# Where the norms of three batches stand, and how the first item's front is cut: a Mamba, attention and expert kernel on one core

## The reference, cut to what matters

```python
x = x + attn(layernorm(x))            # two Mamba blocks, x is (4, 512, 256)
x = x + xattn(layernorm(x), ctx)      # cross attention
x = x + ffn(layernorm(x))             # shared expert and top-2 of 8 experts

# attn, for each of 2 layers:
xz = rmsnorm(x) @ in_w.T;  xb, z = split(xz)
xb = silu(conv4(xb) + cb)             # causal, 4 taps, 512 channels
delta, Bm, Cm = split(xb @ xp_w.T)    # 16 + 16 + 16
delta = softplus(delta @ dtw.T + dtb)
dA = exp(delta[..., None] * -exp(a_log));  mi = delta * Bm * xb
v = 0.6 * v + mi;  h = dA * h + v;  y = (h * C).sum(states)   # along the sequence
x = x + ((y + dp * xb) * silu(z)) @ out_w
```

## Time and profile before

| | us |
|---|---|
| median of three runs | 1530.66 |
| lowest, highest | 1529.70, 1532.19 |
| the profiled execution | 1527.98 |
| its span in the trace | 1526.5 |
| TensorE busy | 1373.7 (90%) |
| VectorE busy | 1056.8 (69%) |
| ScalarE busy | 898.0 (59%) |
| GpSimd busy | 926.8 (61%) |
| first scan starts | 73.8 |
| last scan ends | 948 |

### The profile page before, as it was taken

How to read it: one execution, slowest core, us unless ns; L and a number is a source line. 1 busy time by engine, 2 the same in 40 slices (tenths; PEclk the granted TensorE clock), 3 DMA queues, 4 the chain that set the end, 5 groups by cost and what they waited for, 6 DMA issues and landing times.

```text
span 1526.5 us, 46972 instructions
## 1 busy us (share of the span) xinstructions
PE 1373.7 (90%) x20570; PEld 972.8 (64%) x20570; DVE 1056.8 (69%) x1339; ACT 898.0 (59%) x1309; POOL 926.8 (61%) x809
## 2 busy tenths in 40 slices
PE   4679999999999999999999987789898887999997
PEld 2357677767767767777777765444434343599996
DVE  3299998798888887887986895676676761522224
ACT  3757767767766776786677663145555565434440
POOL 1269898989989989989989968500303000045441
PEclk8789999999999999999999998889999999999999
DMA  4111222221322212221221354540606001512225
GB/s 139 48 56 59 86 86 85 86 84 60 113 85 85 82 62 85 85 87 61 82 86 68 145 135 127 94 104 1 112 14 111 0 1 61 223 53 69 67 67 182
DMA packets 41498, 127.28 MB, mean 83 GB/s; under 512 B 8784, under 2 KB 21584, under 8 KB 32848
## 3 DMA queue, kind: packets, MB, share of 16 engines
q1 hardware_dynamic: 34736, 108.28, 21.8%
q0 software_dynamic: 6048, 14.95, 3.7%
q10 hardware_dynamic: 512, 1.05, 0.4%
HBM read 97.90 MB, written 9.57 MB: 70 GB/s over the span
## 4 chain that ended last, share of the span: by engine, by line
PE 47%; DVE 27%; ACT 10%; issue 8%; POOL 3%; DMA 3%; SPq 1%; DVEq 0%; ACTq 0%
DVE hst L783 12%; PE psum L635 6%; PE psum L614 4%; PE psum L1301 4%; PE psum L1713 4%; PE psum L1725 4%; DVE overlay L683 3%; DVE w_early L783 3%; PE psum L1283 2%; PE psum L576 2%; ACT dA L919 2%; PE psum L516 2%; POOL hst L990 2%; PE psum L1655 2%; PE psum L1267 2%
## 5 line engine op out<-in xcount | busy, mean ns | idle before, releaser
L990 POOL TENSOR_TENSOR hst<-hst,cb 128x512 f32<-128x512 f32 x399 | 510.9, 1304 | 99.0 <-DVE hst L783 84.2
L783 DVE TENSOR_TENSOR_SCAN hst<-dA,psum 128x512 f32<-128x512 f32 x399 | 463.4, 1201 | 119.5 <-PE psum L635 119.3
L614 PE MATMUL psum<-ident,hst 128*128 128x128 f32 x1596 | 238.2, 284 | 15.3 <-POOL hst L990 12.6
L919 ACT ACTIVATE dA<-delta,alog 128x512 f32<-128x512 f32 x256 | 177.7, 718 | 84.7 <-DVE hst L783 64.7
L614 PEld LDWEIGHTS psum<-ident,hst 128*128 128x128 f32 x1596 | 176.1, 143 | 62.4 <-issue 21.1
L919 ACT ACTIVATE dA<-xres,alog 128x512 f32<-128x512 f32 x256 | 176.3, 718 | 63.2 <-DVE hst L783 49.6
L1422 DVE TENSOR_REDUCE nmax<-psum 128x2 f32<-128x1024 f32 x128 | 154.7, 1220 | 57.4 <-PE psum L1267 57.1
L1351 ACT ACTIVATE pT<-psum 128x1024 f32<-128x1024 f32 x128 | 127.9, 1024 | 103.6 <-PE psum L1287 80.3
L635 PE MATMUL psum<-filt,c_early 64*64 64x86 f32 (+1 forms) x6144 | 147.3, 242 | 19.8 <-DVE hst L783 11.0
L635 PEld LDWEIGHTS psum<-filt,c_early 64*64 64x64 f32 x6144 | 126.7, 136 | 57.3 <-issue 38.6
L635 PE MATMUL psum<-filt,uT 64*64 64x86 f32 (+1 forms) x6144 | 145.1, 239 | 14.8 <-DVE hst L783 7.6
(11 more groups left out here) (231 smaller groups left out, 2108.9 us busy)
## 6 DMA issues: line engine op xcount, KB each, us to landing
cb<-c_rows SPq DMA_DIRECT2D x64, 1024.0 KB, 4.8
qk_first<-w_early SPq DMA_DIRECT2D x64, 64.0 KB, 2.4
qk<-part SPq DMA_DIRECT2D x64, 64.0 KB, 2.8
w_up<-up_dram SPq DMA_DIRECT2D x8, 512.0 KB, 7.5
w_down<-down_dram SPq DMA_DIRECT2D x8, 512.0 KB, 13.2
w_up<-y_choice SPq DMA_DIRECT2D x8, 512.0 KB, 6.7
qk<-part POOLq DMA_DIRECT2D x48, 64.0 KB, 5.1
qk_first<-part SPq DMA_DIRECT2D x40, 64.0 KB, 2.4
```

The costliest lines, as they stand in the source:

```text
L614: m = pe.matmul(psum[:, Y0 + et % EP, t * P:(t + 1) * P], hst(i)[:, t * P:(t + 1) * P], ident[:], start=n == 0 and t == 0, stop=n == NSTAT ...
L783: dve.tensor_tensor_scan(hst(i), a, v, 0.0, ALU.mult, ALU.add).then_inc(scan_done, 1)
L919: act.activation(dA[:, a % NDA, :], delta[k % 2][:, et, :], ACT.Exp, scale=alog[:, k // B, et, n:n + 1]).then_inc(decay_done, 1)
L990: pool.tensor_tensor(h, h, cb[:, q % 2, state_of(i)[1] % GN, :], ALU.mult).then_inc(g_done, 1)
```

## The change

`plan_norms` goes, and its work is put into `plan_first`. x_stats of batches 1 to 3 and x_aggr of both groups come on VectorE behind its last u. Both x_roots come on ScalarE behind the u copies, the x_recs behind them on VectorE, and one x_scale ahead of the copies of each of e1, e2 and e3. Silu of item 0 is four instructions, one for each channel tile; each waits for its convolution alone, and the xp products of a tile wait for its silu. `rates` comes straight behind silu. The chunk-end pieces of item 0 are shared: ScalarE copies those of even g, VectorE those of odd g (e1 three and three; e2 two 16x512, one 16x256 and one 16x512 on ScalarE, one 16x512 and one 16x256 on VectorE; e3 two and one). e2, e3 and the first filter products wait for VectorE's copies by a new semaphore `ends_dve`. Decays 0 to 2 stand on ScalarE between its e1 and e2 copies. Item 1's front takes the steps of the later items: xs at step 0, xn from step 2, p at steps 6, 9, 12, 14.

```diff
@@ plan_first
-                put("act", "silu")
+                for m in range(ET):
+                    put("act", "silu", m)
+                put("act", "rates")
@@
-                put("act", "rates")
@@
                     put("dve" if m % 2 else "pool", "u", m)
+                for b in range(1, B):
+                    put("dve", "x_stats", b)
+                for g in range(2):
+                    put("dve", "x_aggr", g)
@@
-                for part in STAGES:
+                for g in range(2):
+                    put("act", "x_roots", g)
+                    put("dve", "x_rec", g)
+                for b, part in zip(range(1, B), STAGES):
+                    put("dve", "x_scale", b)
                     for n in range(len(STAGES[part])):
                         put("pe", part, n)
                     s += 1
                     for n in range(len(STAGES[part])):
                         put("act", part, n)
+                        put("dve", "ends", (part, n))
+                    if part == "e1":
+                        put("act", "decays")
                     s += 1
@@ plan_front
-            def plan_front(k, at, start):
+            def plan_front(k, at):
-                xn_at = 2 if k > 1 else start + 2
-                p_at = (6, 9, 12, 14) if k > 1 else range(start + 5, start + 5 + ET)
+                xn_at, p_at = 2, (6, 9, 12, 14)
@@ pe_side, xp
-                    pe.wait_ge(xbs_done, k + 1)
+                    if k:
+                        pe.wait_ge(xbs_done, k + 1)
@@
+                        if k == 0:
+                            pe.wait_ge(*((xbs_first, kt + 1) if kt < ET - 1 else (xbs_done, 1)))
@@ pe_side, e2 and e3
+                        if k == 0:
+                            pe.wait_ge(ends_dve, 1 if what == "e2" else 3)
@@ pe_mamba
+                        if k == 0:
+                            pe.wait_ge(ends_dve, 4)
@@ dve_side
+                elif what == "ends":
+                    part, n = j
+                    r0, ends_of = STAGES[part][n]
+                    dve.wait_ge(bank_full, filled(k, part, len(STAGES[part]) - 1))
+                    for g, end, half in [x for x in ends_of if x[0] % 2]:
+                        cols = slice(0, DI) if half is None else slice(half * HS, (half + 1) * HS)
+                        to, c = (r0, end + 1) if end < NCH - 1 else (KT, 0)
+                        i = dve.tensor_copy(uT[par][to:to + NSTATE, c, cols], bank(k, part, n)[g * BC:g * BC + NSTATE, cols])
+                    i.then_inc(ends_dve, 1)
@@ act_side
+                elif what == "silu" and k == 0:
+                    act.wait_ge(bank_dve, emptied_by("dve", k, "p", j))
+                    act.activation(xbs[par][:, j, NSTATE:NSTATE + S], uw[:, j, NSTATE:NSTATE + S], ACT.Silu).then_inc(xbs_first if j < ET - 1 else xbs_done, 1)
@@
-                    for g, end, half in ends_of:
+                    for g, end, half in act_ends(k, ends_of):
@@
+                elif what == "decays":
+                    for a in range(AHEAD - 1):
+                        act_decay(a)
@@
+            def act_ends(k, ends_of):
+                return [x for x in ends_of if x[0] % 2 == 0] if k == 0 else ends_of
@@ act_mamba
-                for a in range(AHEAD - 1):
-                    act_decay(a)
```

More of the change, by code:

```diff
@@ L269, in build @@
                 sem(n) for n in ("tap_done", "xs_done", "conv_done", "bend_done", "clip_done", "delta_done", "rms_done", "scan_done", "alog_neg"))
-            xbs_done, sz_done, exp_done, splus_done, sq_done, log_done, root_exp, decay_done, alog_exp, u_first = (
-                sem(n) for n in ("xbs_done", "sz_done", "exp_done", "splus_done", "sq_done", "log_done", "root_exp", "decay_done", "alog_exp", "u_first"))
+            xbs_done, sz_done, exp_done, splus_done, sq_done, log_done, root_exp, decay_done, alog_exp, u_first, xbs_first, ends_dve = (
+                sem(n) for n in ("xbs_done", "sz_done", "exp_done", "splus_done", "sq_done", "log_done", "root_exp", "decay_done", "alog_exp", "u_first", "xbs_first", "ends_dve"))
             steps = {e: {} for e in ("pe", "dve", "act", "pool")}
@@ L410, in plan_mid @@
                     steps["pool"].setdefault((k, (50, 57)[e]), []).append((k, "gate", e))
-            def plan_norms(at, s, g):
-                def put(engine, *name):
-                    steps[engine].setdefault((at, s), []).append((0,) + name)
-                for b in X_GROUPS[g]:
-                    put("dve", "x_stats", b)
-                    s += b > 1
-                put("dve", "x_aggr", g)
-                s += 2 + g
-                put("act", "x_roots", g)
-                s += 2
-                put("dve", "x_rec", g)
-                for b in X_GROUPS[g]:
-                    put("dve", "x_scale", b)
-                    s += 1
-                return s
             def plan_attention(at):
@@ L452, in build @@
             for k in range(NI):
-                s = 0
                 if k:
                     plan_back(k - 1, k, LAG - 2)
-                else:
-                    s = plan_norms(k, 1, 0)
-                    plan_norms(k, TILES - 16, 1)
                 plan_mid(k)
                 if k + 1 < NI:
-                    plan_front(k + 1, k, s)
+                    plan_front(k + 1, k)
                 else:
```

## The result

| | before | after |
|---|---|---|
| median, us | 1532.05 (8 runs, 1527.10 to 1536.68) | 1522.86 (8 runs, 1517.63 to 1525.67) |
| ratio | | 0.9932, 95% interval 0.9914 to 0.9950 |
| the profiled execution, us | 1527.98 | 1523.77 |
| first scan starts | 73.8 | 71.9 |
| item 0 | 115.8 | 102.6 |

The change is faster by 9.2 us in the medians; 1513.5 was forecast. The table says at once that this small gain is a sum of larger ones: item 0 gained 13.2 us, the front only 1.9, and six later items lost 1.84 each, 11.2 together. The change wasn't meant to touch those. Taken with item 7 (0.1 us lost) that leaves the 3.8 us between the ends of the last scans; with 0.5 us behind them, where nothing was changed, it is the 4.2 us between the two profiled executions.

A forecast was written before the change was run, and what follows sets the result against it. The front was taken as one dependency chain with no engine full, item 0's first and last scans as held by VectorE's norms. Gains 6.1 + 8.0 + 3.1 = 17.2 us off 1530.66 gave 1513.5, range 1507.5 to 1523.

The forecast's parts named there:

- Every later item repeats item 1's work: Items after item 0: they stay unchanged, item 1 at 108.9 us, so savings in front and item 0 reach the end.
- Silu by tile and rates: Front: silu per tile and rates moved behind it save 3.16 us at the dbc copies plus 1.60 at the exponentials.
- z: Front, z products and silu: may hold the u copies; charged 0.25 us, bounded 0 to 4.3.
- Norms in the front: Front: norms of batches 1 to 3 hide, roots under e1's products; without that cover they cost 1.9 us.
- Copies on two engines, decays between: Front's chunk-end copies: sharing them between ScalarE and VectorE saves 0.3, 0.7 and 0.6 us in the three stages.
- First scan at 67.7: End of the front: first scan starts 6.1 us earlier, at 67.7; wrong beyond 65 to 71.
- rival 1: Front: z, the clock or contended scaling leaves a gain of 2 us, not 6.1; 1517.5 us; chance 0.12.
- Item 0's first 16 scans: Start of item 0: without norm work 29.1 us instead of 37.1, a gain of 8.0, bounds 4 to 9.6.
- Last 16: End of item 0: without norms 25.9 us instead of 29.0, TensorE late next; gain 3.1, bounds 1.5 and 4.
- Rival 3: Opening of item 0: gaps keep TensorE at 1.2 GHz, 26 us more; 1539.5 us; chance 0.04.
- Rival 2: Item 0's first scans: TensorE bound them, not norms; gain 2 to 3 us, not 8; 1519 us; chance 0.07.
- rival 4: Front: statistics held, roots late, so norms only move there, 6 us on the chain; 1519.5 us; chance 0.05.

The follow-up runs named there:

- e1: The changed kernel with its list of PSUM banks starting as 1, 0, 2, 3, 4, 5: 1511.74 us median, ratio 0.9866.
- e2: The kernel before with its list of PSUM banks starting as 0, 1, 2, 4, 5, 3: 1540.88 us median, ratio 1.0053.
- e7: e3 with one silu over four tiles and rates between clip and exp, as in the kernel before: 1515.69 us profiled.
- e10: e8 with the norms of batches 1 to 3 back in item 0, at the steps of the kernel before: 1524.75 us profiled.
- e9: e3 with the front's side work reordered: decays and roots under products, VectorE's copies ahead of scalings, batch 3's scaling at step 20: 1507.37 us median, ratio 0.9834.
- e6: e3 with all chunk-end copies of item 0 on ScalarE: 1513.45 us profiled.
- e5: e3 with decays 0 to 2 and their table load behind the last chunk-end copies again, as in the kernel before: 1514.63 us profiled.
- e3: e1 plus 60 transposes that nothing reads in TensorE's idle gaps of item 0's front: 1509.82 us median, ratio 0.9853.
- e8: e3 with item 1's front at the steps of the kernel before (xs at 6, input products at 11 to 14): 1510.65 us profiled.
- e11: The kernel before, unedited, in another profiled execution: 1538.19 us.

## Why the prediction was right, and where it was not

Direction and range held: 1522.86 lies in 1507.5 to 1523, at its very end. That the range held is luck. What cost most, the deal of banks, had no part in the sum, and the measured median lies 0.14 us inside the upper end; a gain of 4.2 us, as between the two profiled executions, would have ended outside. The sum didn't hold, 17.2 forecast and 9.2 measured, and the step that failed isn't one of the sum's terms but a condition of it.

- *"Every later item repeats item 1's work, so what item 0 and the front save should arrive at the end."* This failed: items 1 to 6 lost 11.2 us. The prediction's last sentence names it, PSUM banks dealt out in another order, but as something that would show the prediction wrong, without a chance or a price. A sentence in the part on the edit of `plan_front` was due: the move changes the order from which banks are dealt, and the waits in all later items hang on that order. The deal can be worked out from the plan without a run. e1 and e2 show it as the cause.
- *Silu by tile and rates:* 4.76 predicted; the dbc copies end at 31.25 instead of 34.59, 3.34 earlier (0.3 of it from an earlier convolution) for the 3.16 of the sum, and e7 has 4.3 to 5.3 at the u products. Right. In the changed profile the u products start only 3.20 earlier, at 47.93: 3.34 + 1.60, less 0.60 for the transposes ahead of the delta products and 1.15 for the delta products, both at half clock. So the clock took 1.75 us of this gain before e1. Ln loads its own table at 39.98 (the row of L874's load above), as in the kernel before. The Trainium skill, page "ScalarE: Activation LUTs", section "Table sets: the hidden batching unit", would have no load there, and the trace decides against it for this kernel.
- *z:* 0.25 predicted, and it ran at a better clock than before (8.64 us for 9.8). Nothing lost.
- *Norms in the front:* the cover held. Statistics 47.7 to 51.7, roots 55.1 to 55.6 under e1's products, e10 within half a microsecond, though only since the decays hold e2's copies anyway (e9: 0.7 us for both). The first scaling took 1.34, the uncontended price that was chosen.
- *Copies on two engines, decays between:* 1.6 predicted at a like clock, 1.74 by the gaps of e6. VectorE's piece of 0.39 to 0.72 was 0.40 and 0.69, and VectorE ended last in e1 as said. That the load and decays behind e3 "lay beside the first filter products" and count nothing is right at half clock (2.13 us for the inputs, 2.0 for load and decay) and 0.8 us wrong at full clock (e5). For the item it is wrong: up to 2.1 us in the first 16 scans (e5), since item 1's xs is queued behind them. The prediction named who waits for the copies, not who is queued behind the decays.
- *First scan at 67.7:* measured 71.9 and 72.0, outside the 65 to 71 that it allowed. This is rival 1 in its clock form, in the delta products, e1 and e2 instead of z: 5.32 + 3.63 us for 2.81 + 2.21 in e1 and e2, and 1.75 more ahead of the u products. Of its two causes the clock was real and the contended scaling was not. At a clock mostly kept it is 65.5 (e3). The 6.1 us were worked out for a clock like that of the profiled execution of before; the sum gave the clock nothing.
- *Item 0's first 16 scans:* 8.0 predicted, 9.2 measured; 29.1 was forecast and 28.0 came, by a floor of 27.5 from VectorE's work, which was busy for 27.69. The prediction gave the earlier steps of item 1's front no share; they have 2.2 (e8). Last 16: 3.1 predicted, 3.5 measured, TensorE late next, as said.
- *Rival 3*, the clock down through item 0: no. It was at 0.97 in the first 28 us. *Rival 2* is refuted by the first third of item 0, which gained 9.2 us and not 2 to 3, *rival 4* by the front, where the first scan came earlier and the statistics and roots lay under other work.

So the account is: front 1.9 to 5.3 by which execution of before one takes, item 0 13 to 16, less 11.2. Against the profiled execution of before it is 13.2 + 1.9 - 11.3 = 3.8 us up to the last scan; against e11, where 102.6 and 71.9 stand beside 118.7 and 77.2, it is 16.1 + 5.3 less 11.2 in items 1 to 6, and 10.5 between the ends of the last scans. The medians' 9.2 lie between. They aren't split up by place, since only single executions are profiled, and e11 at 1538.19 is itself 6 us above the median.

## What to carry to other kernels

When buffers are dealt out from a plan, an edit of the plan in one place changes who waits for whom everywhere behind it: work out the deal before and after, compare for each user whom it waits for, and if it differs, try another start of the list before judging the edit. A gain in a part that runs once is small beside a wait of one microsecond in a part that repeats. And one profiled execution has one course of the clock: two of the same kernel before reading a difference of a few microseconds in a stretch where TensorE has gaps.

## What the runs showed of the hardware

The granted clock of TensorE takes another course through a chain with gaps in each execution of the same kernel: the same front took 73.8 and 77.2 us, the same delta products 2.6 and 3.78. In the two executions of the changed kernel it fell at 53.2 and at 47.9, and e1's products took 5.32 us both times. The Trainium skill, page "TensorE: Matmul & The Clock Gate", section "Part 1: The HAM clock gate (the "warmup" mystery)", has the gate follow how busy the array was, with windows that run free of the kernel's start; the differing places of the steps agree with that. With sixty transposes in the gaps (8.8 us of TensorE in all) it stayed at 2.4 GHz from 37.7 to 61.6 us in e3, and e1's products took 2.78 us in seven executions of seven. In the front of e3 they paid for themselves; at the last scan 0.3 us of it was left. With 103 of them in the kernel before the clock was still down from 30.9 to 41.2 and from 51.4 to 54.8 us, and up from there to 82.1; why not sooner stays open.
